# A state-space scan on Trainium2: GpSimd makes one of the four scalings of dt\*x by B in each step

## The chip, the cores and the metric

The kernel runs on one core of one Trainium2 chip. The metric is the device time of one execution in microseconds, the median of several runs. The core has five engines with a queue each, and a queue is worked off in order: TensorE (PE in the rows, its weight loads PEld), VectorE (DVE), ScalarE (ACT), GpSimd (POOL) and SyncE (SP), which issues DMAs. They are tied to each other by semaphores.

## What is computed

A layer of a sequence model: layernorm, a bidirectional state-space block, layernorm and sum, then attention and a mixture of eight experts. The change lies in the state-space block alone. Cut to that:

```
u: [2, 2048, 256];  x, z: [2, 2048, 512];  16 states per channel
xc = silu(causal_conv4(x));  dt, B, C = split(xc @ xp_w.T);  dt = softplus(dt @ dt_w.T + dt_b)
for t:                                       # forwards and, on flipped rows, backwards
    h = exp(dt[t] * A) * h + (dt[t] * xc[t]) * B[t]     # for each channel and state n
    y[t] = sum_n h[.., n] * C[t, n] + D * xc[t]
```

## The kernel before

The program is seven stages one after the other: projection of the inputs, the scan (`scan_channels`), mixing and qkv, attention, routing, the experts, and the combination. The change is in the scan.

The scan works in 16 units: two batches, four chunks of 512 positions, two directions. A unit holds 512 channels as four tiles of 128 partitions, and makes 16 steps, one per state n. A step is a chain over four engines:

- ACT scales the transposed product dt\*x (`dtxT`, positions on the partitions) by B for state n, four tiles of 128x512 (`spread_b`, L536 to L540), into `dBxT[n % 2]`; and makes four decays `dA = exp(dt * A)` (`decay`, L531 to L534). It works a step ahead of the scans: the scaling for step n+1 is queued at step n, and waits until PE has read the step that used the same buffer.
- PE transposes the scaled tiles back into PSUM (`inject`, L749 to L757), four transposes for each of the four channel tiles, into a ring of three banks `bx`.
- DVE runs the recurrence over 512 positions in one instruction per channel tile (`scan`, L661 to L672), from `dA` and `bx` into `hh[n % 2]`.
- POOL multiplies the result by C (L471), in two halves of two channel tiles each, into `hC[n % 2]`, and between them copies the last column of the scan into `state` (L469).
- PE adds the products to the accumulator (`add`, L759 to L768), eight channel tiles, that is two steps, behind the injects.

Between the steps of a unit the front of the next unit is made, in pieces placed by hand at fixed steps: the convolution on PE (L703) with its output on ACT (L485), the SiLU with two table loads on ACT (L490, L491, in step 3), the projections on PE (L713, L727) with their outputs on ACT (L498, L502, L510, L511), the softplus on ACT, POOL (L447, queued at step 9) and DVE (L644 and L650, after the scans of step 10), the product with x on DVE (L655, after step 11), and the transposes to `dtxT` on PE (L735) with their output on ACT (L529). All these pieces go through one PSUM bank `fr`, so PE and ACT take turns on it. PE's inject waits for ACT's scalings by the semaphore `bd_ok`.

Of the kernel before, what the change touches and what calls it, by code (L numbers as in the profile page):

```python
# [17 lines left out]
ALU = mybir.AluOpType  # L18
# [10 lines left out]
DT = DI // P  # L29
NS = 16  # L30
# [7 lines left out]
JT = C // P  # L38
# [92 lines left out]
def hold(eng, k):  # L131


    eng.sem_inc(k["passed"], 1)
# [207 lines left out]
def scan_channels(nc, k, xin, crows, y, convw, convb, xpw, dtw, dtb, alog, dskip):  # L342

    with Stage(nc, "scan") as s:
# [13 lines left out]
        dtxT = [s.sb(f"dtxT{i}", [P, JT, DI]) for i in range(2)]  # L358
# [3 lines left out]
        bt = [s.sb(f"bt{i}", [P, JT, 2 * NS]) for i in range(2)]  # L362
        dBxT = [s.sb(f"dBxT{i}", [P, JT, DI]) for i in range(2)]
# [8 lines left out]
        loaded_x = s.sems("loaded_x0", "loaded_x1")  # L372
        loaded_c = s.sems("loaded_c0", "loaded_c1")
        (loaded_w, diags, a_raw, a_ready, fr_mm, fr_out, silu_ok, e_ok, u_ok, v_ok, d_ok, ln_ok, dt_ok, front_ok,
         stored_c, bd_ok, bx_mm, da_ok, h_ok, hc_ok, saved, zeroed, acc_ok, skip_ok, y_out, y_stored) = s.sems(
            "loaded_w", "diags", "a_raw", "a_ready", "fr_mm", "fr_out", "silu_ok", "e_ok", "u_ok", "v_ok", "d_ok",
            "ln_ok", "dt_ok", "front_ok", "stored_c", "bd_ok", "bx_mm", "da_ok", "h_ok", "hc_ok", "saved", "zeroed",
            "acc_ok", "skip_ok", "y_out", "y_stored")
        NW = 7
        SUB = NS * DT  # L380
# [4 lines left out]
        FR_CONV, FR_PROJ, FR_BT, FR_DT, FR_NEXT, FR_TURN, FR_ALL = 0, 2, 3, 4, 8, 10, 14  # L385

        HELD_HC, HELD_H, HELD_SAVED, HELD_BX = 16, 8, 2, 8
        LAG = 8

        def bank(j):  # L390
            return 1 if j == SUB - 1 else j % 3

        def bank_free(j):
            back = 1
            while bank((j - back) % SUB) != bank(j):
                back += 1
            return j - back + 1 + HELD_H
# [7 lines left out]
        @block.sync  # L405
        def _(sp):
            for dst, src in ((cw[:, :, :, :], convw), (cb[:, :, :], convb), (db[:, :, :], dtb), (dk[:, :, :], dskip),
                             (an[:, :, :, :], alog), (wp[:, :, :, :], xpw), (wrk[:, :, :], dtw)):
                sp.dma_start(dst, src).then_inc(loaded_w, 16)

            def load_x(b, c, d):
                at = c * C if d == 0 else (NC - 1 - c) * C + HALO
                sp.dma_start(xw[d][:, :, :], xinv[b, :, :, at:at + C + HALO]).then_inc(loaded_x[d], 16)

            for d in range(2):
                load_x(0, 0, d)
            with sp.Fori(0, B) as b:
                for c in range(NC):
                    for d in range(2):
                        f = (b * NC + c) * 2 + d  # L420

                        sp.wait_ge(fr_mm, f * FR_ALL + 4)
                        hold(sp, k)
                        if c + 1 < NC:
                            load_x(b, c + 1, d)
                        else:
                            load_x(1 - b, 0, d)

                        sp.wait_ge(fr_out, f * FR_ALL + 5)
                        sp.dma_start(crows[d], pr[RANK:RANK + NS, :]).then_inc(stored_c, 16)  # L430
                        sp.wait_ge(stored_c, f * 16 + 16)
                        for g in range(NS // GROUP):

                            sp.wait_ge(hc_ok, (f * NS + g * GROUP - 2 * GROUP) * 2 + 2 * GROUP + HELD_HC)
                            sp.dma_start(cbc[g % 2][:, :, :],
                                         crows[d:d + 1, g * GROUP:(g + 1) * GROUP, :].broadcast_to([P, GROUP, C])
                                         ).then_inc(loaded_c[g % 2], 16)

        @block.gpsimd
        def _(pool):  # L440
            for i in range(2):
                pool.memset(hC[i][:, :, :], 0.0).then_inc(hc_ok, HELD_HC // 2)
            pool.sem_inc(saved, HELD_SAVED)

            def front_relu_and_e(d, g):
                pool.wait_ge(e_ok, g + 1)
                pool.tensor_tensor(dt[d][:, :, :], dt[d][:, :, :], ee[:, :, :], ALU.add).then_inc(v_ok, 1)  # L447

            front_relu_and_e(0, 0)
            with pool.Fori(0, B) as b:  # L450

                pool.wait_ge(saved, b * (2 * NC * NS) + HELD_SAVED)
                hold(pool, k)
                pool.memset(state[:, :, :, :], 0.0).then_inc(zeroed, 1)
                with pool.Fori(0, NC) as c:
                    for d in range(2):
                        f = (b * NC + c) * 2 + d
                        for n in range(NS):
                            q = f * NS + n
                            h, rows = hh[n % 2], cbc[n // GROUP % 2][:, n % GROUP, :]  # L460
                            edge = C - 1 if d == 0 else 0
                            if n % GROUP == 0:
                                pool.wait_ge(loaded_c[n // GROUP % 2], f * 32 + (n // GROUP // 2) * 16 + 16)
                            for half in range(2):
                                ms = slice(2 * half, 2 * half + 2)
                                pool.wait_ge(h_ok, q * DT + 2 * half + 2 + HELD_H)
                                if half:
                                    hold(pool, k)
                                    pool.tensor_copy(state[:, d, n, :], h[:, :, edge]).then_inc(saved, 1)  # L469
                                pool.wait_ge(acc_ok, q * DT + 2 * half + 2)  # L470
                                pool.tensor_tensor(hC[n % 2][:, ms, :], h[:, ms, :],  # L471
                                                   rows.unsqueeze(1).broadcast_to([P, 2, C]), ALU.mult
                                                   ).then_inc(hc_ok, 1)
                            if n == 9:
                                front_relu_and_e(1 - d, f + 1)

        @block.scalar
        def _(act):
# [55 lines left out]
                               ).then_inc(da_ok, 1)  # L534

            def spread_b(d, n):  # L536
                for j in range(JT):
                    last = act.activation(dBxT[n % 2][:, j, :], dtxT[d][:, j, :], ACT.Copy,  # L538
                                          scale=bt[d][:, j, NS + n:NS + n + 1])
                last.then_inc(bd_ok, 1)  # L540
# [30 lines left out]
            for m in range(DT):  # L571
                decay(0, 0, 0, m)
            act.wait_ge(fr_out, 14)
            spread_b(0, 0)

            def unit(b, c, d, f):
                o, g, first = 1 - d, f + 1, f * FR_ALL + 16
                for n in range(NS):
                    q = f * NS + n
                    dn, at = (d, n + 1) if n + 1 < NS else (o, 0)  # L580
                    if n + 1 == NS:
                        act.wait_ge(fr_out, first + FR_ALL)
                    act.wait_ge(bx_mm, q * DT + HELD_BX)
                    spread_b(dn, at)
                    if n == 2:
                        for half in range(2):
# [102 lines left out]
        def _(pe):  # L689
# [59 lines left out]
            def inject(d, f, j):  # L749
                n, m = j // DT, j % DT  # L750
                if m == 0:
                    pe.wait_ge(bd_ok, f * NS + n + 1)
                pe.wait_ge(h_ok, f * SUB + bank_free(j))
                for t in range(JT):
                    last = pe.transpose(bx[bank(j)][:, t * P:(t + 1) * P], dBxT[n % 2][:, t, m * P:(m + 1) * P],  # L755
                                        k["ident"][:, :])
                last.then_inc(bx_mm, 1)  # L757
# [1496 lines left out]
```

## Time and profile before

| | us |
|---|---|
| median of 3 runs | 4661.33 (4647.94 to 4668.38) |
| the profiled execution | 4669.25 |
| its span, first to last instruction | 4667.7 |
| busy in the span: PE, DVE, ACT, POOL | 3683.8, 2845.9, 2754.8, 1718.3 |

The page gives shares over the whole span, and the stages have different limits. The scan runs from about 248 to 2068 us of the span. What a change in it is worth is read from the rows of that stretch: which engine is busy in it, and which wait ends last before an instruction that stands idle. In the rows, "idle before" or a bracket is the idle time of the engine just before the instruction, with what ended it.

### The profile page before, as it was taken

How to read it: one execution, taken by the hardware profiler on the slowest of the kernel's cores; microseconds unless marked ns; L12 is line 12 of the kernel's file. 1: busy time of each engine (PE TensorE's matmuls, PEld its weight loads, DVE VectorE, ACT ScalarE, POOL GpSimd, SP SyncE). 2: the span in 40 equal slices, each digit the busy share in tenths (PEclk: the TensorE clock that was granted, in tenths of full speed). 3: DMA queues.
4: the chain of work that ended last, by engine and by line, in shares of the span. 5: the costliest groups of instructions: out<-in, count | busy, mean ns of one | idle time of the engine just before them, and what ended most of it. 6: DMA issues, size and time to landing. Idle time of an engine off the chain costs nothing. (4 is left out here: it accounts for less than half of the span.)

```text
span 4667.7 us, 68770 instructions
## 1 busy us (share of the span) xinstructions
PE 3683.8 (79%) x20726; PEld 2252.4 (48%) x20726; DVE 2845.9 (61%) x4186; ACT 2754.8 (59%) x4377; POOL 1718.3 (37%) x1132
## 2 busy tenths in 40 slices
PE   8488878888888888866776888888888885499990
PEld 4266666666666666644553222222222223366660
DVE  4268777787778777756665666666666665411105
ACT  3289898888989898964663455555555551011110
POOL 0067777777777777754342000000000002300006
PEclk9789999899989898988876899999999997699995
DMA  6311111111111111124544001000010103312215
GB/s 208 110 46 55 56 56 56 64 55 56 55 56 63 51 61 56 56 90 147 200 159 156 17 24 27 24 24 20 24 27 24 27 17 112 125 52 71 71 44 184
DMA packets 151517, 329.76 MB, mean 71 GB/s; under 512 B 17443, under 2 KB 92310, under 8 KB 136656
## 3 DMA queue, kind: packets, MB, share of 16 engines
q1 hardware_dynamic: 97392, 229.08, 14.5%
q10 hardware_dynamic: 39760, 51.81, 3.2%
q0 software_dynamic: 13968, 43.97, 2.8%
q8 instruction: 200, 3.28, 0.3%
q14 instruction: 197, 1.61, 0.1%
HBM read 216.45 MB, written 110.91 MB: 70 GB/s over the span
## 5 line engine op out<-in xcount | busy, mean ns | idle before, releaser
L671 DVE TENSOR_TENSOR_SCAN scan_hh<-scan_dA,scan_state,scan_bx 128x512 f32<-128x512 f32 x1024 | 1247.4, 1265 | 399.9 <-PE scan_bx L755 354.4
L471 POOL TENSOR_TENSOR scan_hC<-scan_hh,scan_cbc 128x1024 f32<-128x1024 f32 x512 | 1208.5, 2370 | 316.7 <-DVE scan_hh L671 243.1
L1403 DVE TENSOR_REDUCE attend_mx<-attend_s 128x1 f32<-128x512 f32 (+1 forms) x1360 | 782.3, 608 | 340.5 <-PE attend_s L1533 221.8
L755 PE MATMUL scan_bx<-kept_ident,scan_dBxT 128*128 128x128 f32 x4096 | 676.7, 291 | 151.2 <-DVE scan_hh L671 125.1
L755 PEld LDWEIGHTS scan_bx<-kept_ident,scan_dBxT 128*128 128x128 f32 x4096 | 521.3, 150 | 417.5 <-issue 209.4
L538 ACT ACTIVATE scan_dBxT<-scan_dtxT,scan_bt 128x512 f32<-128x512 f32 x1028 | 656.1, 712 | 89.4 <-PE scan_bx L755 89.2
L533 ACT ACTIVATE scan_dA<-scan_dt,scan_an 128x512 f32<-128x512 f32 x1028 | 655.5, 712 | 0.0
L765 PE MATMUL scan_acc<-kept_ident,scan_hC 128*128 128x128 f32 x4128 | 652.3, 286 | 1.3 <-POOL scan_hC L471 1.3
L1533 PE MATMUL attend_s<-attend_kt,attend_qt 96*128 96x512 bf16 (+1 forms) x1360 | 483.7, 374 | 145.6 <-DVE attend_mx L1403 74.3
L1497 ACT ACTIVATE attend_full<-attend_s 128x1024 f32<-128x1024 f32 x384 | 391.9, 1025 | 338.5 <-PE attend_s L1560 334.6
L765 PEld LDWEIGHTS scan_acc<-kept_ident,scan_hC 128*128 128x128 f32 x4128 | 521.7, 150 | 1.6 <-POOL scan_hC L471 1.6
L1381 POOL DMA_DIRECT2D scratch_attnT<-attend_out x16 | 7.9, 496 | 1341.1 <-DVE attend_out L1437 1341.1
L1533 PEld LDWEIGHTS attend_s<-attend_kt,attend_qt 96*128 96x128 bf16 x1360 | 129.5, 97 | 644.7 <-DVE attend_mx L1403 532.9
L703 PE MATMUL scan_fr<-scan_xw,scan_diag 128*128 128x512 f32 x560 | 303.6, 631 | 94.5 <-ACT scan_xc L485 39.0
L1560 PE MATMUL attend_s<-attend_qt,attend_kt 99*128 99x512 bf16 (+3 forms) x1284 | 360.7, 353 | 0.0
L1501 ACT ACTIVATE attend_diag<-attend_s 128x512 f32<-128x512 f32 (+3 forms) x512 | 192.7, 440 | 196.4 <-PE attend_s L1563 179.6
L2018 DVE TENSOR_TENSOR experts_yt<-experts_py,experts_b2t 128x256 f32<-128x256 f32 x64 | 27.2, 425 | 425.0 <-PE experts_py L2065 425.0
L2032 ACT ACTIVATE experts_hid<-experts_ph,experts_b1t 128x512 f32<-128x512 f32 x128 | 87.5, 687 | 249.8 <-PE experts_ph L2056 249.7
L2056 PE MATMUL experts_ph<-experts_xT,experts_w1t 128*128 128x512 f32 x512 | 224.7, 598 | 13.0 <-DVE experts_xT L2013 11.3
L2065 PE MATMUL experts_py<-experts_w2t,experts_hid 128*128 128x256 f32 x1024 | 222.3, 379 | 0.0
L2065 PEld LDWEIGHTS experts_py<-experts_w2t,experts_hid 128*128 128x128 f32 x1024 | 194.6, 190 | 29.9 <-issue 3.8
L1578 PE MATMUL attend_pv<-attend_full,attend_vs 128*32 128x512 f32 x1536 | 204.6, 605 | 0.0
(218 smaller groups left out, 4604.8 us busy)
## 6 DMA issues: line engine op xcount, KB each, us to landing
scan_cbc<-scratch_crows SPq DMA_DIRECT2D x64, 1024.0 KB, 4.7
scratch_qk<-mix_heads ACTq DMA_DIRECT2D x64, 384.0 KB, 9.7
scan_xw<-scratch_xin SPq DMA_DIRECT2D x18, 1030.0 KB, 7.3
scratch_y<-scan_uu ACTq DMA_DIRECT2D x17, 1024.0 KB
attend_qt<-scratch_qk SPq DMA_DIRECT2D x34, 384.0 KB, 3.9
attend_kt<-scratch_qk SPq DMA_DIRECT2D x34, 384.0 KB, 4.7
mix_yf<-scratch_y SPq DMA_DIRECT2D x10, 1024.0 KB, 8.4
mix_yb<-scratch_y SPq DMA_DIRECT2D x10, 1024.0 KB, 12.0
```

The lines of the kernel that those rows point to most:

```text
L471: pool.tensor_tensor(hC[n % 2][:, ms, :], h[:, ms, :], rows.unsqueeze(1).broadcast_to([P, 2, C]), ALU.mult).then_inc(hc_ok, 1)
L533: act.activation(dA[n % 2][:, m, :], dt[d][:, m, :], ACT.Exp, scale=an[:, d, m, n:n + 1]).then_inc(da_ok, 1)
L538: last = act.activation(dBxT[n % 2][:, j, :], dtxT[d][:, j, :], ACT.Copy, scale=bt[d][:, j, NS + n:NS + n + 1])
L671: dve.tensor_tensor_scan(hh[n % 2][:, m, r], dA[n % 2][:, m, r], bx[bank(j)][:, r], state[:, d, n, m:m + 1], ALU.mult, ALU.add).then_inc(h ...
L703: last = pe.matmul(fr[:, :], diag[:, d, m, j, :], xw[d][:, m, o:o + C], start=j == 0, stop=j == TAPS - 1)
L755: last = pe.transpose(bx[bank(j)][:, t * P:(t + 1) * P], dBxT[n % 2][:, t, m * P:(m + 1) * P], k["ident"][:, :])
L765: last = pe.matmul(acc[:, j, m * P:(m + 1) * P], hC[n % 2][:, m, j * P:(j + 1) * P], k["ident"][:, :], start=a == 0, stop=False, is_transp ...
L1403: dve.tensor_reduce(mx[:, t, c:c + 1], s1[v % 2][:, 0:w], AX_X, ALU.max).then_inc(s1_read, 1)
L1497: last = act.activation(buf[:, 2 * half:2 * half + 2, :], s2[st % 2][:, :, :], ACT.Exp)
L1533: last = pe.matmul(s1[v % 2][:, 0:w], qt[j1][0:STACK, t * P:(t + 1) * P], kt_[j1][0:STACK, c * C:c * C + w], start=True, stop=c < t // JT)
L1560: last = pe.matmul(s2[st % 2][:, r, o:], kt_[j][:, kt * P:(kt + 1) * P], qt[j][:, qc * C + o:(qc + 1) * C], start=True, stop=quad < qc)
L2065: last = pe.matmul(py[j % 2][:, :], hid[ch][:, f, (j % JT) * P:(j % JT + 1) * P], w2t[i][:, f, :], start=f == 0, stop=f == FT - 1)
```

## The change

Of the four tiles of `dBxT` in each step ACT makes three, and POOL makes the last (`JT - 1`), as a `tensor_scalar` of 128x512 with the column of B as its scalar. POOL queues it between its two products of a step, and for two steps ahead, while ACT queues its three for one step ahead. Before it POOL waits until PE has made all four injects of the step (the buffer is then free), and for the last two steps of a unit until the next unit's `dtxT` is there. The first two are made ahead of the loop. PE's inject waits for a second semaphore, `bd_pool`, beside `bd_ok`.

```diff
             front_relu_and_e(0, 0)
+            pool.wait_ge(fr_out, 14)
+            hold(pool, k)
+            for n in range(2):
+                spread_b(0, n)
             with pool.Fori(0, B) as b:
...
+            def spread_b(d, n):
+                pool.tensor_scalar(dBxT[n % 2][:, JT - 1, :], dtxT[d][:, JT - 1, :],
+                                   bt[d][:, JT - 1, NS + n:NS + n + 1], None, ALU.mult).then_inc(bd_pool, 1)
...
                                 pool.tensor_tensor(hC[n % 2][:, ms, :], h[:, ms, :],
                                                    rows.unsqueeze(1).broadcast_to([P, 2, C]), ALU.mult
                                                    ).then_inc(hc_ok, 1)
+                                if half == 0:
+                                    if n + 2 == NS:
+                                        pool.wait_ge(fr_out, f * FR_ALL + 16 + FR_ALL)
+                                    pool.wait_ge(bx_mm, (q + 1) * DT + HELD_BX)
+                                    hold(pool, k)
+                                    spread_b(d if n + 2 < NS else 1 - d, (n + 2) % NS)
...
             def spread_b(d, n):
-                for j in range(JT):
+                for j in range(JT - 1):
                     last = act.activation(dBxT[n % 2][:, j, :], dtxT[d][:, j, :], ACT.Copy,
...
                     pe.wait_ge(bd_ok, f * NS + n + 1)
+                    pe.wait_ge(bd_pool, f * NS + n + 1)
```

## Rows read from the trace of the kernel before

**Rows 1.** The page's engines over the whole span: busy us, share, instructions.

```profile
PE 3683.8 (79%) x20726; PEld 2252.4 (48%) x20726; DVE 2845.9 (61%) x4186; ACT 2754.8 (59%) x4377; POOL 1718.3 (37%) x1132
```

**Rows 2.** Stretches: one unit, and a run of ACT in it; the columns are the first line's.

```profile
core 0: us, PE busy (x) PEld busy (x) DVE busy (x) ACT busy (x) POOL busy (x), PEclk, DMA share, GB/s
929.26:1042.20 112.94, 96.00 (x616) 76.56 (x615) 88.88 (x68) 98.55 (x152) 83.96 (x49) 0.90 0.15 56
935.73:979.68 43.95, 36.86 (x274) 30.40 (x272) 34.08 (x28) 43.89 (x67) 33.70 (x22) 1.00 0.13 49
```

**Rows 3.** DVE's group L671, 300 to 1980 us; L469's durations min/median/max, whole span.

```profile
L671 DVE TENSOR_TENSOR_SCAN scan_hh<-scan_dA,scan_state,scan_bx 128x512 f32<-128x512 f32 x947 | 1153.5, 1265 | 346.6 <-PE scan_bx L755 304.2 <-ACT scan_dA L533 31.2 <-POOL scan_state L469 6.5
...
L469 POOL COPY scan_state<-scan_hh x256: 177/188/2289, 257.4 to 2065.5; 128x4 f32<-128x4 f32 x128
```

**Rows 4.** Waits, 300 to 1980 us: waiter, waited for: us in total, times, longest.

```profile
PE scan_fr L727 <- ACT scan_dt L511: 53.4, 29, 2.6
PE scan_fr L713 <- ACT scan_xc L490: 27.5, 14, 2.2
PE scan_bx L755 <- ACT scan_dBxT L538: 18.1, 23, 1.1
DVE scan_hh L671 <- ACT scan_dA L533: 31.2, 19, 4.8
```

**Rows 5.** Timeline: ACT in the run of rows 2, then DVE in steps 12 to 14.

```profile
935.73 2.56 ACT L538 ACTIVATE scan_dBxT<-scan_dtxT,scan_bt 128x512 f32<-128x512 f32 x4 [4.00 <-PE scan_bx L755]
...
973.53 1.94 ACT L538 ACTIVATE scan_dBxT<-scan_dtxT,scan_bt 128x512 f32<-128x512 f32 x3
...
1020.59 10.64 DVE L671 TENSOR_TENSOR_SCAN scan_hh<-scan_dA,scan_state,scan_bx 128x512 f32<-128x512 f32 x9
```

**Rows 6.** Timeline: PE and DVE where they stand behind ACT.

```profile
956.87 1.09 PE L713 MATMUL scan_fr<-scan_xc,scan_wp 128*96 128x512 f32 x2 [2.18 <-ACT scan_xc L490]
958.44 1.28 DVE L671 TENSOR_TENSOR_SCAN scan_hh<-scan_dA,scan_state,scan_bx 128x512 f32<-128x512 f32 x1 [1.59 <-PE scan_bx L755]
960.75 0.65 PE L755 MATMUL scan_bx<-kept_ident,scan_dBxT 128*128 128x128 f32 x4 [1.05 <-ACT scan_dBxT L538]
961.62 1.28 DVE L671 TENSOR_TENSOR_SCAN scan_hh<-scan_dA,scan_state,scan_bx 128x512 f32<-128x512 f32 x1 [1.90 <-PE scan_bx L755]
979.73 2.07 PE L727 MATMUL scan_fr<-scan_pr,scan_wrk 64*128 64x512 f32 x2 [2.16 <-ACT scan_dt L511]
982.88 1.28 DVE L671 TENSOR_TENSOR_SCAN scan_hh<-scan_dA,scan_state,scan_bx 128x512 f32<-128x512 f32 x1 [4.13 <-PE scan_bx L755]
```

**Rows 7.** Timeline: POOL and DVE from step 8 to the softplus of step 10.

```profile
989.12 2.36 POOL L471 TENSOR_TENSOR scan_hC<-scan_hh,scan_cbc 128x1024 f32<-128x1024 f32 x1 [2.29 <-DVE scan_hh L671]
1000.08 4.56 POOL L447 TENSOR_TENSOR scan_dt<-scan_dt,scan_ee 128x2048 f32<-128x2048 f32 x1
1004.58 2.39 POOL L471 TENSOR_TENSOR scan_hC<-scan_hh,scan_cbc 128x1024 f32<-128x1024 f32 x1
1004.74 4.37 DVE L644 SCALAR_TENSOR_TENSOR scan_ee<-scan_uu,scan_dt 128x2048 f32<-128x2048 f32 x1 [0.87 <-POOL scan_dt L447]
1006.88 2.28 POOL L469 COPY scan_state<-scan_hh 128x4 f32<-128x4 f32 x1
1009.12 2.34 POOL L471 TENSOR_TENSOR scan_hC<-scan_hh,scan_cbc 128x1024 f32<-128x1024 f32 x1
1009.22 4.40 DVE L650 SCALAR_TENSOR_TENSOR scan_dt<-scan_dtx,scan_ee 128x2048 f32<-128x2048 f32 x1
```

**Rows 8.** POOL's instructions by line over the whole span: busy us, mean ns.

```profile
L962 POOL TENSOR_TENSOR mix_rest<-mix_rot,mix_parts 128x512 f32<-128x512 f32 x32 | 36.9, 1153 | 171.4 <-DVE mix_parts L1070 171.4
L1375 POOL MEMSET attend_vs<- 128x512 f32 x2 | 1.1, 525 | 0.0
L120 POOL TENSOR_SCALAR_AFFINE_SELECT kept_ident<-kept_ident 128x128 f32<-128x128 f32 x1 | 0.3, 282 | 0.2 <-POOL kept_one L117 0.2
L112 POOL MEMSET kept_ident<- 128x128 f32 x1 | 0.2, 205 | 0.3 <-POOLq L2247 0.3
```

More of the change, by code:

```diff
@@ L374, in scan_channels @@
         (loaded_w, diags, a_raw, a_ready, fr_mm, fr_out, silu_ok, e_ok, u_ok, v_ok, d_ok, ln_ok, dt_ok, front_ok,
-         stored_c, bd_ok, bx_mm, da_ok, h_ok, hc_ok, saved, zeroed, acc_ok, skip_ok, y_out, y_stored) = s.sems(
+         stored_c, bd_ok, bd_pool, bx_mm, da_ok, h_ok, hc_ok, saved, zeroed, acc_ok, skip_ok, y_out, y_stored) = s.sems(
             "loaded_w", "diags", "a_raw", "a_ready", "fr_mm", "fr_out", "silu_ok", "e_ok", "u_ok", "v_ok", "d_ok",
-            "ln_ok", "dt_ok", "front_ok", "stored_c", "bd_ok", "bx_mm", "da_ok", "h_ok", "hc_ok", "saved", "zeroed",
+            "ln_ok", "dt_ok", "front_ok", "stored_c", "bd_ok", "bd_pool", "bx_mm", "da_ok", "h_ok", "hc_ok", "saved", "zeroed",
             "acc_ok", "skip_ok", "y_out", "y_stored")
```

## The prediction

> **What bounds the kernel now.** I read the page's table of engines first [rows 1]: TensorE is busiest over the whole span, but that is a mean over seven stages, and the change touches one, the scan. So the second view is the table of stretches [rows 2]. One unit of the scan (16 steps; 929.26 is the first scan of its step 0) takes 112.94 us, with ACT busy 98.6, PE 96.0, DVE 88.9 and POOL 84.0. There are 16 units, so 1 us per unit is 16 us of the kernel. No engine is full over a unit. The third view, the groups of the stage by line [rows 3], tells how they wait: DVE's scans lost 346.6 us, 304.2 of it to PE's inject (L755), 31.2 to ACT and 6.5 to POOL. The fourth, the waits [rows 4], asks what PE waits for in its turn. The rows where PE or DVE stands for ACT add up to 53.4 + 27.5 + 18.1 + 31.2 = 130.2 us in 300 to 1980, that is 14.9 units: 8.7 us per unit.
>
> The timeline of one unit shows where. ACT starts a run at 935.73, when PE frees the buffer, and does not idle until 979.68: 43.89 of 43.95 us busy [rows 2, 5]. In this run it makes seven steps' scalings and decays, and between them the conv output, the evacuation, the SiLU with two table loads, the projections. Three places hang on it [rows 6]: PE's projection waits 2.18 us for the SiLU (956.87), PE's inject of step 5 waits 1.05 us for the scaling (960.75), and PE's dt product waits 2.16 us for ACT's dt output (979.73), behind which DVE stands 4.13 us (982.88). So in steps 1 to 7 ACT sets the pace. From 985 on PE (the convolutions between injects) and POOL do, and in steps 12 to 14 DVE runs nine scans without a gap [rows 5].
>
> **The change, part by part.**
>
> *What ACT loses.* One of four scalings per step. A group of three lasts 1.94 us and one of four 2.56 [rows 5], so 0.61 us a step, 9.8 us a unit. It is worth something only where ACT is late. (a) From 935.73 to the scaling for step 5 there are four groups (for steps 2, 3, 4, 5): ACT comes 4 x 0.61 = 2.45 us earlier. The SiLU comes after three, 1.84 us earlier, against a stall of 2.18. The stalls behind them on DVE, 1.59 and 1.90 us before the scans at 958.44 and 961.62, hold that much: I take 2.4 us. (b) By the dt output seven groups have been saved, 4.3 us, of which 2.4 have been passed on in (a) already; the other 1.9 come off PE's stall of 2.16 at 979.73. Steps 5 and 6 in between are PE's and DVE's own, so the shift passes through unchanged. (a) and (b) are 4.3 us per unit. The rest of ACT's 9.8 falls in steps 8 to 15 and 0, where others end last: I cost it at nothing.
>
> *What POOL gains: the price p of one tensor_scalar, 128x512 f32.* The trace shows none. The nearest rows [rows 8]: a product of the same size with two inputs 1.153 us, a memset of that size, with no input, 0.525 us. A one-input instruction of 128x128 takes 0.282 us against 0.205 for the memset of that size; those 0.077 us, times four for the columns, on top of 0.525 give 0.83 us. I take 0.83, the one-input row being nearest in kind, with 0.53 and 1.15 as ends. The Trainium skill (GPSIMD Engine Reference) speaks against the change: its introduction calls GpSimd the wrong choice for ordinary elementwise arithmetic, and its section Performance versus the Vector engine has a tight loop over 512 elements at 769 ns. No row here shows that loop; by it the sum below would be better by 0.2 us per unit.
>
> *Whether POOL carries it.* POOL's 84.0 us become 84.0 + 16 x 0.83 = 97.3 of the new unit's 108 (102.4 with 1.15), so it becomes the busiest engine. A plain step costs it two products, a copy and p: 2 x 2.35 + 0.15 + 0.83 = 5.7 us, against 4.8 for DVE's four scans: in steps 12 to 14 POOL falls behind by 0.9 us a step. It may: the scaling is made two steps ahead. POOL's first product of a step can start after the step's second scan, and the inject that wants the scaling must be done six scans (7.2 us) later; less 0.65 for the inject and 3.2 for product and scaling, 3.3 us are in reserve. Three such steps use 2.7 of them, and step 0 (PE's convolutions) gives them back. The new wait for the injects (bx_mm) stands in POOL's queue before the scaling, the state copy and the second product; those need the same step's last two scans, which need the same injects, so it delays nothing that could have run. PE gets one more semaphore a step. For both I take 0.4 us per unit off.
>
> *Steps 8 to 10, where POOL is late already* [rows 7]. From 989.12 POOL makes steps 8 and 9 and the sum (L447, 4.56 us), for which DVE's subtraction (L644) waits. This one and the next (L650) read two SBUF tiles, take 4.37 and 4.40 us, and end 2.15 us after a POOL product ends (1006.97 and 1011.46); the state copy between them lasts 2.28 us where the median one lasts 0.19 [rows 3]. So these DVE instructions and POOL's exclude each other whole, and whichever stands waiting goes next. The Trainium skill (SBUF — State Buffer, Who interferes with whom) says the same: a VectorE instruction with two SBUF inputs and a GpSimd instruction that reads SBUF block each other for their whole length, and the order of issue decides who waits. The trace agrees, with the 2.28 us. Now L650 ends at 989.12 + 24.5. With the change: two steps of 4.85 + p, the sum 4.5, a product 2.35, L644 2.15, then the scaling (p) gets in ahead of L650 in place of copy and product (2.35), then 2.15: 20.85 + 3p. That is 23.3 for p = 0.83: 1.2 us gained (2.1 with 0.53, 0.2 with 1.15). The displaced product runs behind L650, 3 us later; PE needs it two steps on, so nothing waits.
>
> **Sum.** 2.4 + 1.9 + 1.2 - 0.4 = 5.1 us per unit, x 16 = 82 us. The profiled execution took 4669.25 us (span 4667.7 and 1.5 around it) and would take 4588; it lies 8 us above the median of the runs, 4661.33. On the median: 4580 us. The ends of p alone give 4.1 and 6.0 us per unit: 4596 and 4565.
>
> **Rivals.**
> 1. *All of ACT's time comes back.* Every stall behind ACT shrinks, the smaller ones too (conv output, decays). For: PE and DVE lose 8.7 us a unit to ACT. Against: steps 8 to 15. Bound 9.8 us per unit: 4505 us; around 4530 as a middle. 12%.
> 2. *The exclusion turns against it.* If the scaling starts just ahead of each of the three two-input DVE instructions of a unit, each waits p more and L650 gains nothing: 5.1 - 1.2 - 3 x 0.83 = 1.4 us, 22 us: 4639. For: POOL is nearly always in an instruction now. Against: at 1009 the scaling displaces a longer product. 10%. The Trainium skill's rule of issue order, named above, would make it so wherever the scaling is issued first.
> 3. *POOL sets the pace and eats the gain.* A lag in steps 11 to 15 that step 0 does not give back, p near 1.3: POOL's 84.0 + 21 = 105, plus 5 us in which it must wait for PE's adds and for ACT's exponential: 110 or more; gain 0 to 2 us: about 4650. For: 97 of 108 us busy in strict order. 12%.
> 4. *Slower: the price.* If the per-partition scalar makes p more than about 1.6 us, POOL's own 84.0 + 16p, with some 3 us of waits it cannot avoid, passes 112.9, and every unit takes what POOL takes. For p = 2.0: 119, 6 us per unit: 4760 us. For: no row shows this instruction. Against: it would cost more than the two-input product of its size [rows 8]. 12%.
> That leaves 54% for the forecast.
>
> **How the numbers follow.** About 0.5% (23 us) is what a measurement of this kernel can tell from no change. Faster: the forecast (54), rival 1 (12), some 5 of rival 2's 10 and 3 of rival 3's 12: 0.74. Same: the rest of those, 0.14. Slower: rival 4, 0.12. The range goes from 4530 (middle of rival 1) to 4645, which holds the forecast, both ends of p, rival 2 and part of 3; left out are rival 4, the far end of 1 and the upper end of 3, some 2 in 10.
>
> **What would show it.** Right: three scalings on ACT per step (1.94 us), 256 on POOL at 0.5 to 1.2 us; the waits of PE for the SiLU (27.5 us) and the dt output (53.4 us) at less than half; a unit of about 108 us, ACT near 89 us busy in it, POOL near 97; L650 shorter than 4.4 us. Wrong: waits of PE's inject for POOL's scaling, of DVE for POOL's copy or products, in sums of over 1 us a unit; a scaling above 1.3 us; the dt stall unchanged, which would mean that something other than ACT's queue held it.

## The result: slower by some 0.6 percent, and what the profile after shows

The changed kernel takes 4688.9 us (median; 4688.6 to 4698.3), the kernel before 4663.2 beside it: the ratio over all runs is 1.0067, 95% interval 1.0052 to 1.0081. The difference is small but clear of the noise. The forecast was 4580 with a range to 4645. The profiled execution has a span of 4687.6 us against 4667.7.

First GpSimd's new instruction by itself (minimum, median and maximum in ns, then its first and last start), with those who waited for it:

```profile
L450 POOL TENSOR_SCALAR scan_dBxT<-scan_dtxT,scan_bt x258: 1552/1574/3768, 235.0 to 2084.1; 128x512 f32<-128x512 f32 x129
...
  PE scan_bx L770: 54.0, 55
```

It lasts 1.55 us where nothing hinders it, and takes 1.51 from its start to the next instruction's. The forecast had 0.83, with 1.15 as its upper end. The stretches of two units (the second begins at the same place of the loop as [rows 2]; columns as there) and GpSimd's queue in the first, in which brackets would show idle time:

```profile
820.40:938.06 117.66, 92.11 (x611) 72.47 (x610) 90.43 (x67) 92.85 (x141) 112.98 (x67) 0.92 0.15 56
938.06:1048.94 110.88, 91.24 (x616) 72.70 (x615) 89.59 (x67) 89.79 (x136) 106.15 (x65) 0.95 0.16 58
```

```profile
823.59 1.55 POOL L450 TENSOR_SCALAR scan_dBxT<-scan_dtxT,scan_bt 128x512 f32<-128x512 f32 x1
825.10 0.18 POOL L477 COPY scan_state<-scan_hh 128x4 f32<-128x4 f32 x1
825.25 4.73 POOL L479 TENSOR_TENSOR scan_hC<-scan_hh,scan_cbc 128x1024 f32<-128x1024 f32 x2
829.97 1.55 POOL L450 TENSOR_SCALAR scan_dBxT<-scan_dtxT,scan_bt 128x512 f32<-128x512 f32 x1
...
888.65 2.36 POOL L479 TENSOR_TENSOR scan_hC<-scan_hh,scan_cbc 128x1024 f32<-128x1024 f32 x1
890.98 4.53 POOL L447 TENSOR_TENSOR scan_dt<-scan_dt,scan_ee 128x2048 f32<-128x2048 f32 x1
```

From 793.9 to 903.9 GpSimd has no idle time at all; a step costs it 6.34 us (scaling to scaling, 823.59 to 829.97 and on). It is busy 106 and 113 us of a unit, where before it had 84 of 113. ACT fell from 98.6 us busy to 90 to 93. VectorE at step 10 of the first unit, to be read against [rows 7]:

```profile
895.62 4.45 DVE L658 SCALAR_TENSOR_TENSOR scan_ee<-scan_uu,scan_dt 128x2048 f32<-128x2048 f32 x1 [4.41 <-POOL scan_dt L447]
900.17 5.91 DVE L664 SCALAR_TENSOR_TENSOR scan_dt<-scan_dtx,scan_ee 128x2048 f32<-128x2048 f32 x1
```

It waits 4.41 us for GpSimd's sum, where it had waited 0.87, and its second subtraction takes 5.91 us, where it had taken 4.40. Over 300 to 1980 us the waits (us in total, times, longest) that answer to [rows 4], and the new ones:

```profile
PE scan_fr L741 <- ACT scan_dt L525: 46.3, 30, 1.9
PE scan_fr L727 <- ACT scan_xc L504: 4.5, 7, 0.8
PE scan_bx L770 <- ACT scan_dBxT L552: 3.7, 8, 0.6
DVE scan_hh L685 <- ACT scan_dA L547: 27.3, 17, 2.0
DVE scan_ee L658 <- POOL scan_dt L447: 50.0, 15, 4.4
PE scan_bx L770 <- POOL scan_dBxT L450: 49.6, 51, 1.8
```

PE and VectorE stood 81.8 us for ACT, where it was 130.2: the stalls that the change aimed at did shrink. In their place stand 99.6 us for GpSimd, of which VectorE's wait for the sum had been 15.9 before, and PE's wait for GpSimd's scaling had not existed. TensorE's clock is no rival for the loss: over 300 to 1980 us its granted share rose (the last three figures are PEclk, DMA share and GB/s; before, then after):

```profile
300.00:1980.00 1680.00, 1378.30 (x9038) 1102.77 (x9038) 1316.97 (x992) 1489.86 (x2273) 1270.64 (x725) 0.92 0.16 57
300.00:1980.00 1680.00, 1341.15 (x8956) 1059.78 (x8957) 1318.58 (x984) 1339.55 (x2025) 1604.00 (x954) 0.94 0.15 57
```

Where in a unit that is, the starts of the first scan of each step tell. The table has the mean us of such stretches over 14 units (all but the first and the last), worked out from the traces, for the two kernels and for those of the experiments (e8 left out):

| | steps 1 to 4 | 5, 6 | 7 to 9 | 10 | 11 to 14 | 15, 0 | sum | median us |
|---|---|---|---|---|---|---|---|---|
| before | 25.2 | 13.5 | 23.2 | 15.5 | 22.0 | 14.3 | 113.7 | 4663 |
| after | 23.7 | 13.5 | 21.5 | 18.4 | 22.4 | 15.0 | 114.4 | 4689 |
| e1, fourth left out | 22.2 | 13.5 | 21.5 | 15.5 | 21.2 | 14.4 | 108.2 | 4583 |
| e2, load alone | 25.0 | 13.5 | 23.3 | 14.5 | 22.4 | 14.6 | 113.3 | 4679 |
| e3, two inputs | 22.4 | 13.5 | 22.2 | 14.0 | 21.2 | 14.2 | 107.4 | 4576 |
| e4, steps 2 to 8 | 22.8 | 13.5 | 22.3 | 15.5 | 21.9 | 14.0 | 110.0 | 4611 |
| e6, two inputs, 2 to 8 | 22.8 | 13.5 | 22.3 | 15.5 | 21.9 | 14.1 | 110.0 | 4612 |
| e7, not 12, 13 | 23.9 | 13.5 | 21.2 | 18.2 | 21.2 | 14.7 | 112.6 | 4657 |
| e9, after second | 24.9 | 13.5 | 21.3 | 17.7 | 25.0 | 14.2 | 116.6 | 4727 |
| e11, order | 23.8 | 13.5 | 21.2 | 15.7 | 23.7 | 14.7 | 112.7 | 4662 |
| e12, sum earlier | 23.7 | 13.5 | 21.6 | 15.0 | 24.3 | 14.8 | 112.9 | 4666 |
| e13, two inputs, sum earlier | 22.3 | 13.5 | 21.1 | 13.7 | 22.0 | 14.1 | 106.6 | 4560 |
| e14, padded | 24.2 | 13.5 | 21.2 | 19.8 | 22.4 | 14.4 | 115.5 | 4703 |

After against before: 1.4 us gained in steps 1 to 4, 1.8 in steps 7 to 9, 2.9 lost in step 10, 1.0 in 11 to 0; 0.8 us a unit lost in all. From the two spans: the scans, first to last, take 1827.2 us in place of 1816.4; the first starts 2.9 later; and GpSimd's last product ends 9.1 us after the last scan in place of 2.7. That is 10.8 + 2.9 + 6.4 = 20.1 of the 19.9 us between the spans. The 2.9 at the start is not seen in the trace of every later kernel and may be chance.

The column for steps 7 to 9 needs care, since TensorE's granted clock moves it. In the changed kernel, in e3 and in e13 each unit takes either 20.6 us there or 22.3 (one of each, from e3 and e13, columns as above):

```profile
1042.79:1065.09 22.30, 18.97 (x110) 13.99 (x109) 14.94 (x14) 19.84 (x29) 20.71 (x16) 0.92 0.28 97
1038.38:1059.00 20.62, 17.30 (x110) 12.32 (x109) 14.67 (x13) 18.16 (x29) 19.93 (x13) 1.00 0.32 105
```

The same 110 instructions keep PE busy 18.97 us in the first, in which the clock stood at its lower level (1.2 in place of 2.4 GHz) for 3.4 us, after PE had stood 1.94 us for ACT's dt output. Every unit of these kernels at a granted clock of 1.00 takes 20.6 us; one with a fall takes 20.6 or 22.3, as it seems by where it falls. Such units are 7 of 14 in the changed kernel, 13 in e3 and 4 in e13 at 22.3 us, so differences in this column between kernels with three scalings on ACT (21.1 to 22.2) are the clock's, not GpSimd's.

### The profile page after: what moved, and what is told of

It is laid out like the page before. It is cut to its first block and busy times, and to the rows that moved or that the text cites. A ratio compares the mean times of both kernels' runs of the same rounds, so it can differ in the third digit from the quotient of the medians.

```text
span 4687.6 us, 69557 instructions
## 1 busy us (share of the span) xinstructions
PE 3654.1 (78%) x20726; PEld 2213.3 (47%) x20726; DVE 2860.1 (61%) x4186; ACT 2601.7 (56%) x4120; POOL 2094.7 (45%) x1390
## 3 DMA queue, kind: packets, MB, share of 16 engines
q1 hardware_dynamic: 97392, 229.08, 14.5%
## 5 line engine op out<-in xcount | busy, mean ns | idle before, releaser
L770 PE MATMUL scan_bx<-kept_ident,scan_dBxT 128*128 128x128 f32 x4096 | 660.9, 286 | 263.5 <-DVE scan_hh L685 200.5
L770 PEld LDWEIGHTS scan_bx<-kept_ident,scan_dBxT 128*128 128x128 f32 x4096 | 504.0, 147 | 533.9 <-DVE scan_hh L685 352.7
L552 ACT ACTIVATE scan_dBxT<-scan_dtxT,scan_bt 128x512 f32<-128x512 f32 x771 | 498.6, 712 | 217.6 <-PE scan_bx L770 217.4
L780 PEld LDWEIGHTS scan_acc<-kept_ident,scan_hC 128*128 128x128 f32 x4128 | 507.3, 147 | 12.3 <-POOL scan_hC L479 7.2
L450 POOL TENSOR_SCALAR scan_dBxT<-scan_dtxT,scan_bt 128x512 f32<-128x512 f32 x258 | 447.5, 1735 | 15.5 <-ACT scan_dtxT L543 15.0
L2012 POOL DMA_DIRECT2D scratch_exp_out<-experts_yt x16 | 12.2, 760 | 486.8 <-DVE experts_yt L2033 486.8
```

What stands on the lines that cost most here:

```text
L450: pool.tensor_scalar(dBxT[n % 2][:, JT - 1, :], dtxT[d][:, JT - 1, :], bt[d][:, JT - 1, NS + n:NS + n + 1], None, ALU.mult).then_inc(bd_po ...
L780: last = pe.matmul(acc[:, j, m * P:(m + 1) * P], hC[n % 2][:, m, j * P:(j + 1) * P], k["ident"][:, :], start=a == 0, stop=False, is_transp ...
```

## The experiments

Two theories stood. PACE: the tensor_scalar is so dear that GpSimd's strict queue sets the pace. EXCLUSION: the harm is in where the scaling stands, at steps 10 and 11, next to VectorE's two-input instructions.

**e1_left_out.** Nobody makes the fourth scaling (the edit against the kernel before).

```diff
+            for i in range(2):
+                pool.memset(dBxT[i][:, JT - 1, :], 0.0).then_inc(bd_pool, 1)
...
-                for j in range(JT):
+                for j in range(JT - 1):
...
+            pe.wait_ge(bd_pool, 2)
```

> Leaves part of the computation out: nobody makes the fourth scaling (its quarter of the buffer is zeroed once), so ACT makes three a step as in the changed kernel and GpSimd has the load it had before. Two theories stand. PACE: a scaling costs GpSimd 1.51 us start to start, so a step costs it 6.34 us and it sets the pace; ACT's saving as such is worth what the prediction had, 4.3 us a unit: 4663 - 16 x 4.3 = 4594 us (4580 to 4605). EXCLUSION: the loss comes from the place of the scaling at steps 10 and 11, where GpSimd and VectorE's two-input instructions shut each other out; it gives about the same here. A third reading, that ACT's saving is worth little because PE and VectorE take over, gives 4640 or more.

Measured: 4583.1 us, 0.9844 of before (0.9825 to 0.9864). ACT's saving alone is worth 77 us by the medians (4.8 us a unit), and by the table, that is by one execution of each, 5.5 us a unit: 3.0 in steps 1 to 4, 1.8 in steps 7 to 9, 0.8 in 11 to 14. The forecast's 4.3 for (a) and (b) was a little low. Step 10 stays at 15.5. PACE and EXCLUSION expected the same here; the third reading falls.

Against e1 the loss of the changed kernel can be read part by part: ACT's saving gives 5.5 us a unit; GpSimd's load takes back 2.9 in step 10 and 3.3 outside it (1.5 in steps 1 to 4, 1.2 in 11 to 14, 0.6 in 15 and 0). What is left is the loss of 0.8 us a unit (by the unrounded figures).

**e3_two_inputs.** The same scaling by another instruction.

```diff
-                pool.tensor_scalar(dBxT[n % 2][:, JT - 1, :], dtxT[d][:, JT - 1, :],
-                                   bt[d][:, JT - 1, NS + n:NS + n + 1], None, ALU.mult).then_inc(bd_pool, 1)
+                pool.tensor_tensor(dBxT[n % 2][:, JT - 1, :], dtxT[d][:, JT - 1, :],
+                                   bt[d][:, JT - 1, NS + n:NS + n + 1].broadcast_to([P, DI]), ALU.mult
+                                   ).then_inc(bd_pool, 1)
```

> GpSimd makes the scaling as a product of two tensors, B broadcast along the free dimension, in place of a tensor_scalar. The kernel before has a two-input product of this size at 1.153 us. PACE: a step costs GpSimd 5.98 us in place of 6.34, it gains 5.9 us a unit on its work and reaches step 8 in time: the forecast's sum at p = 1.15, 4.1 us a unit, less 0.5 for start and end: 4605 us (4595 to 4640). EXCLUSION: as many GpSimd instructions stand between VectorE's two-input instructions as in the changed kernel, so the time stays within 10 us of its 4689.

Measured: 4576.3 us, 0.9831 (0.9810 to 0.9851): 113 us less than the changed kernel, with as many instructions at the same places. PACE had the direction, and its range ended 19 us too high; EXCLUSION as put, that the place and the number of the instructions make the loss, falls. GpSimd's instruction in this kernel, and the two engines at step 10:

```profile
L450 POOL TENSOR_TENSOR scan_dBxT<-scan_dtxT,scan_bt x258: 1029/1047/3107, 232.7 to 1967.4; 128x512 f32<-128x512 f32 x129
```

```profile
966.28 2.38 POOL L480 TENSOR_TENSOR scan_hC<-scan_hh,scan_cbc 128x1024 f32<-128x1024 f32 x1
966.45 4.37 DVE L659 SCALAR_TENSOR_TENSOR scan_ee<-scan_uu,scan_dt 128x2048 f32<-128x2048 f32 x1 [1.23 <-POOL scan_dt L447]
968.61 3.10 POOL L450 TENSOR_TENSOR scan_dBxT<-scan_dtxT,scan_bt 128x512 f32<-128x512 f32 x1
970.92 2.94 DVE L665 SCALAR_TENSOR_TENSOR scan_dt<-scan_dtx,scan_ee 128x2048 f32<-128x2048 f32 x1
971.66 2.25 POOL L478 COPY scan_state<-scan_hh 128x4 f32<-128x4 f32 x1
973.87 2.35 POOL L480 TENSOR_TENSOR scan_hC<-scan_hh,scan_cbc 128x1024 f32<-128x1024 f32 x1
```

1.03 us in place of 1.55. At step 10 the sequence of the prediction's part on steps 8 to 10 runs as written: product, first subtraction, scaling (held for 2 us), second subtraction, which now takes 2.94 us in place of 4.40, then copy and product. All 16 units have it, and step 10 is 1.4 us shorter than in e1. Against the changed kernel step 10 is 4.3 us shorter: VectorE waits 2.0 us less for the sum, and its two subtractions take 2.3 us less. So shutting out is still a part of the 113 us, by the order of the instructions and not by their number.

**e4_steps_2_to_8.** GpSimd makes the tensor_scalar for steps 2 to 8 alone.

```diff
+        BY_POOL = (2, 3, 4, 5, 6, 7, 8)
...
-                                if half == 0:
+                                if half == 0 and (n + 2) % NS in BY_POOL:
...
-                for j in range(JT - 1):
+                for j in range(JT - 1 if n in BY_POOL else JT):
```

> GpSimd makes the fourth scaling only for steps 2 to 8, where ACT was behind; ACT makes all four for the others. PACE: GpSimd carries 1.51 us more in seven steps that were longer than 6.34 us on the mean, catches up before step 10, and ACT's 4.3 us a unit stay: 4600 us (4590 to 4625). EXCLUSION: no scaling stands at steps 10 and 11, so the same. If neither: GpSimd's load in steps 0 to 6 alone puts it late at step 10, 4650 or more.

Measured: 4611.2 us, 0.9909 (0.9886 to 0.9931). Where GpSimd has room afterwards, even the dear instruction pays. Both theories had expected that; the reading that falls is that the load in steps 0 to 6 alone makes it late.

**e7_not_12_13.** As e4, with all steps but 12 and 13.

```diff
+        BY_POOL = (0, 1, 2, 3, 4, 5, 6, 7, 8, 9, 10, 11, 14, 15)
```

> GpSimd makes the fourth scaling for all steps but 12 and 13, which are the two queued between its products in steps 10 and 11, next to VectorE's two-input instructions; ACT makes four for those two. EXCLUSION: the loss of step 10 goes, 2.9 us a unit and more: 4600 to 4630 us. PACE: GpSimd still runs at 6.34 us a step from step 0 to 9 without idle time and reaches the sum late; only the two scalings less count, 1 to 2 us a unit: 4655 to 4675 us.

Measured: 4657.0 us, 1.0001 (0.9989 to 1.0014). With no scaling at step 10, that step still takes 18.2 us: VectorE waits for the sum, up to 4.6 us.

```profile
DVE scan_ee L659 <- POOL scan_dt L448: 53.7, 15, 4.6
```

PACE's 4655 to 4675 holds, and the loss at step 10 does not need the scaling there. Nor does e3's sequence come: in 15 of the 16 units the copy and the second product go ahead of the first subtraction, and the pair of subtractions takes 9.2 us.

**e8_prices.** A price list, from a single run.

```diff
...
+                if n % 8 == 0:
+                    made = pool.tensor_scalar(out[:, :], x, by, None, ALU.mult)
+                if n % 8 == 1:
+                    made = pool.tensor_scalar(out[:, :], x, 0.5, None, ALU.mult)
...
```

> A price list for GpSimd. ACT makes all four scalings as before, and GpSimd makes one more instruction at the place of the change into a spare buffer that nobody reads, in eight forms that alternate with the step: tensor_scalar with a per-partition scalar over 512, 256 and 128 columns, the same with a constant over 512, a product of two tensors over 512 with B broadcast, one with two full tensors, one broadcast over 256, and a copy over 512. COLUMNS: the tensor_scalar is dear for each column (1.51 us at 512, near 0.8 at 256, 0.45 at 128, the constant as dear). SCALAR: fetching the per-partition scalar is a fixed cost (512, 256 and 128 columns less than 0.5 us apart, the constant near 0.8). The product with a broadcast stays at 1.0 us start to start. Its time is of little use: between 4663 and 4740 us.

Measured: 4656.6 us (one run), below the expected range. The durations of the forms (ns, minimum, median, maximum; the larger ones were held up by VectorE):

```profile
L454 POOL TENSOR_SCALAR scan_spare<-scan_dtxT,scan_bt x33: 1553/1567/1602, 233.9 to 2043.3; 128x512 f32<-128x512 f32 x33
L456 POOL TENSOR_SCALAR scan_spare<-scan_dtxT x33: 1478/1490/1526, 235.4 to 2049.6; 128x512 f32<-128x512 f32 x33
L458 POOL TENSOR_SCALAR scan_spare<-scan_dtxT,scan_bt x32: 912/924/945, 258.6 to 1998.4; 128x256 f32<-128x256 f32 x32
L460 POOL TENSOR_TENSOR scan_spare<-scan_dtxT,scan_bt x32: 1029/1040/1068, 264.8 to 2004.5; 128x512 f32<-128x512 f32 x32
L462 POOL TENSOR_TENSOR scan_spare<-scan_dtxT x32: 1276/2310/3341, 272.8 to 2014.8; 128x512 f32<-128x512 f32 x32
L464 POOL COPY scan_spare<-scan_dtxT x32: 599/1652/2693, 278.8 to 2025.1; 128x512 f32<-128x512 f32 x32
L466 POOL TENSOR_TENSOR scan_spare<-scan_dtxT,scan_bt x32: 602/615/639, 284.1 to 2032.5; 128x256 f32<-128x256 f32 x32
L468 POOL TENSOR_SCALAR scan_spare<-scan_dtxT,scan_bt x32: 592/602/636, 291.3 to 2037.9; 128x128 f32<-128x128 f32 x32
```

COLUMNS holds: (1.553 - 0.912) / 256 = 2.5 ns for each column of the tensor_scalar, 128 to 512; a constant in place of the scalar saves 0.075 us, so SCALAR falls. The product with B broadcast costs (1.029 - 0.602) / 256 = 1.7 ns a column, the copy of 512 columns 0.60 us at best.

**e2_both.** GpSimd's load alone: its tensor_scalar goes to a spare buffer, ACT makes four.

```diff
-                pool.tensor_scalar(dBxT[n % 2][:, JT - 1, :], dtxT[d][:, JT - 1, :],
+                pool.tensor_scalar(spare[n % 2][:, :], dtxT[d][:, JT - 1, :],
...
-                for j in range(JT - 1):
+                for j in range(JT):
```

> GpSimd's load alone: it makes the tensor_scalar as in the changed kernel, with the same waits and PE waiting for it, but into a spare buffer, and ACT makes all four scalings as before. With ACT's three and no load on GpSimd the time was 4583 us, 77 below before. ADDITIVE: the load costs 25 + 77 us by itself: 4660 + 102 = 4762 us. PACE: GpSimd's 6.34 us a step and ACT's run are two limits of which the later counts, so ACT's fourth scaling adds only where GpSimd is not behind (step 4 and step 7, some 1.5 to 3 us a unit): 4710 to 4740 us.

Measured: 4679.3 us, 1.0038 (1.0026 to 1.0051). Both readings fail: the load costs 17 us, and taking a quarter of the scalings from ACT as well makes the kernel no faster (1.0067 of before against 1.0038). The table shows why. ACT's saving is there in the changed kernel (23.7 against 25.0 in steps 1 to 4, 21.5 against 23.3 in steps 7 to 9), but step 10 takes 18.4 us against 14.5. VectorE comes to it sooner, GpSimd does not: it is later by comparison, and VectorE waits 1.3 us a unit more for the sum. The larger part, 2.6 us, is the order of the instructions behind it. With the load alone the order at step 10 was e3's in all units (first subtraction, scaling, second subtraction: the good order from here on),

```profile
1004.96 4.37 DVE L659 SCALAR_TENSOR_TENSOR scan_ee<-scan_uu,scan_dt 128x2048 f32<-128x2048 f32 x1 [1.61 <-POOL scan_dt L448]
1007.15 3.61 POOL L451 TENSOR_SCALAR scan_spare<-scan_dtxT,scan_bt 128x512 f32<-128x512 f32 x1
1009.43 2.59 DVE L665 SCALAR_TENSOR_TENSOR scan_dt<-scan_dtx,scan_ee 128x2048 f32<-128x2048 f32 x1
```

and in the changed kernel in none. In 12 of its 16 units the scaling went ahead of the first subtraction (here at 784.00, not held up):

```profile
781.79 5.03 DVE L658 SCALAR_TENSOR_TENSOR scan_ee<-scan_uu,scan_dt 128x2048 f32<-128x2048 f32 x1 [2.17 <-POOL scan_dt L447]
784.00 1.55 POOL L450 TENSOR_SCALAR scan_dBxT<-scan_dtxT,scan_bt 128x512 f32<-128x512 f32 x1
786.92 4.40 DVE L664 SCALAR_TENSOR_TENSOR scan_dt<-scan_dtx,scan_ee 128x2048 f32<-128x2048 f32 x1
```

and in four, as in the unit of the result's section, the copy and the product went ahead of the second. The pair takes 7.1 us in the good order, 9.5 and 10.4 in these.

**e11_order.** The first subtraction ahead of the scaling by force, in the changed kernel.

```diff
                                     pool.wait_ge(bx_mm, (q + 1) * DT + HELD_BX)
+                                    if n == 10:
+                                        pool.wait_ge(d_ok, f + 2)
```

> The changed kernel with one wait more: at step 10 GpSimd makes its scaling only when VectorE's first subtraction of the softplus (L658) is done. In the changed kernel the two subtractions took 9.5 us together in 12 of 16 units and 10.4 in four, because the scaling or the copy and the second product went ahead of one of them; with the load alone (ACT making all four) the order was subtraction, scaling, subtraction in all units, and they took 7.1. ORDER: that order comes back by force, 2.4 to 3.3 us a unit: 4689 - 43 = 4646 us (4635 to 4665). PACE: GpSimd, which sets the pace, loses the 2 us for which it now waits, and gives the gain back in the steps behind: 4675 to 4695 us.

Measured: 4661.8 us, 1.0008 (0.9997 to 1.0020). What came is not quite the order of e2: both subtractions go ahead of the scaling, in all units, and the second has nothing in its way.

```profile
996.89 4.36 DVE L660 SCALAR_TENSOR_TENSOR scan_ee<-scan_uu,scan_dt 128x2048 f32<-128x2048 f32 x1 [2.47 <-POOL scan_dt L447]
1001.36 2.29 DVE L666 SCALAR_TENSOR_TENSOR scan_dt<-scan_dtx,scan_ee 128x2048 f32<-128x2048 f32 x1
```

Step 10 shrinks by 2.7 us to 15.7, and step 11 grows by 1.3: GpSimd, which had to wait, is later, and VectorE's product with x now takes 3.7 us in place of 2.4. So 27 us of the 43 stay, at the upper end of ORDER's range. The order has a share of its own in the loss, about as large as the whole loss, but it does not bring ACT's 77 us back.

**e12_sum_earlier.** The sum one step sooner.

```diff
-                            if n == 9:
+                            if n == 8:
                                 front_relu_and_e(1 - d, f + 1)
```

> The changed kernel with GpSimd's sum for the softplus (L447) queued after step 8 in place of step 9; ACT's exponential is done by then (881.26 in one unit, where the second product of step 8 starts at 882.32). LATE AT ONE PLACE: VectorE's wait for the sum, 50 us in 15 units, goes: 4689 - 16 x 3.3 = 4636 us (4620 to 4650). PACE: GpSimd's work of a unit is the same, and what it does sooner here makes its products late there: 4670 to 4695 us.

Measured: 4665.6 us, 1.0016 (1.0004 to 1.0028). VectorE no longer waits for the sum, and step 10 loses 3.4 us; steps 11 to 14 take 2.0 us more, and PE's wait for GpSimd's scaling grows from 49.6 to 111.0 us:

```profile
PE scan_bx L770 <- POOL scan_dBxT L450: 111.0, 85, 4.2
```

Between the two expectations: more than half of step 10's gain is given back in the steps behind. The order at step 10 is mixed here; in eight of the 16 units the two subtractions take 10.9 to 13.3 us together.

**e9_after_second.** The tensor_scalar behind the second product.

```diff
-                                if half == 0:
+                                if half == 1:
                                     if n + 2 == NS:
```

> The changed kernel with GpSimd's tensor_scalar queued after the second product of the step, not between the two; all else as it was. PLACE: if the loss came from holding up the state copy and the second product, it goes: 4600 to 4650 us. PACE: the same work in one strict queue, 6.34 us a step, and the scaling comes 2.5 us later for PE: 4685 to 4720 us.

Measured: 4726.9 us, 1.0134 (1.0109 to 1.0159). That is above both ranges. The place between the products was not the fault; the later one costs another 38 us, 2.7 us a unit of it in steps 11 to 14.

**e6_two_inputs_2_to_8.** e3's instruction for e4's steps.

```diff
+        BY_POOL = (2, 3, 4, 5, 6, 7, 8)
...
+                pool.tensor_tensor(dBxT[n % 2][:, JT - 1, :], dtxT[d][:, JT - 1, :],
...
+                                if half == 0 and (n + 2) % NS in BY_POOL:
```

> GpSimd makes the fourth scaling as a product of two tensors, and only for steps 2 to 8. Made for all steps it took 4576 us. If GpSimd, busy 96% there, was still a bound somewhere, leaving it nine steps less helps: 4560 to 4575. If every step's saving on ACT counted and step 10 gained from the scaling that stands between VectorE's two subtractions (14.04 us against 15.47 without it, in the two kernels run), it loses that: 4576 + 16 x 1.4 = 4598 us, up to 4605.

Measured: 4611.5 us, 0.9888 (0.9861 to 0.9914), the same as e4, and a little above the second reading. For these steps the price did not matter, and the nine others are worth 35 us with the cheap one, 1.4 a unit of it at step 10.

**e14_padded.** e3 made as dear as the change.

```diff
+                pool.tensor_tensor(spare[n % 2][:, :], dtxT[d][:, JT - 1, 0:DI // 2],
+                                   bt[d][:, JT - 1, NS + n:NS + n + 1].broadcast_to([P, DI // 2]), ALU.mult
+                                   ).then_inc(pad_ok, 1)
                 pool.tensor_tensor(dBxT[n % 2][:, JT - 1, :], dtxT[d][:, JT - 1, :],
...
+                                    pool.wait_ge(pad_ok, q + 1)
```

> The fourth scaling on GpSimd as a product of two tensors for all steps (4576 us), and ahead of each a second product of 256 columns into a buffer that nobody reads. In the price list such a product takes 0.556 us start to start and the scaling 0.982, together 1.54, against 1.51 for the tensor_scalar. PRICE: only the time on GpSimd counts: 4689 us as in the changed kernel (4670 to 4705). FORM: the tensor_scalar does harm in another way than by its length, as by the order at step 10: 4575 to 4640 us.

Measured: 4703.1 us, 1.0086 (1.0065 to 1.0106). With 0.56 us more on GpSimd in each step, e3's whole gain of 85 us turns into a loss of 37, and step 10 goes from 14.0 to 19.8 us. It is the time on GpSimd that does it, without any tensor_scalar. One thing is not kept apart: at step 10 the padding is also one instruction more that can go ahead of VectorE.

**e13_two_inputs_sum_earlier.** e3 with e12's edit.

```diff
+                pool.tensor_tensor(dBxT[n % 2][:, JT - 1, :], dtxT[d][:, JT - 1, :],
...
-                            if n == 9:
+                            if n == 8:
```

> The fourth scaling on GpSimd as a product of two tensors for all steps (4576 us), and the sum queued after step 8. VectorE waited 1.2 us a unit for the sum there. If only that wait goes: 4576 - 20 = 4556 us. If the scaling then falls before another of VectorE's two-input instructions and the order that was good at step 10 is lost: 4575 to 4600 us.

Measured: 4560.5 us, 0.9795 (0.9778 to 0.9812), the fastest of all, and near the first reading's 4556, but not by its mechanism. VectorE's wait for the sum is gone, yet step 10 gains only 0.4 us a unit: e3's good order is lost in all 16 units, and the two subtractions take 8.4 us in place of 7.4. Steps 11 to 14 give 0.8 back. What makes up the difference is steps 7 to 9, 1.1 us a unit or 18 us, and there it is TensorE's clock (four units at 22.3 us in place of 13). Whether the earlier sum brings the better clock about is not shown. GpSimd is busy 96% of the stretch from 300 to 1980 us in this kernel too:

```profile
300.00:1980.00 1680.00, 1411.62 (x9495) 1123.35 (x9494) 1377.94 (x1040) 1416.61 (x2140) 1605.65 (x1012) 0.95 0.17 61
```

## Why the prediction was wrong

- *What bounds the kernel, and (a) and (b).* Right. Steps 1 to 7 stood behind ACT; without any load on GpSimd (e1) steps 1 to 9 gave 4.8 us a unit, where the prediction had 4.3, and steps 11 to 14 another 0.8 that it had costed at nothing. In the changed kernel the waits for the SiLU fell from 27.5 to 4.5 us and those for the scaling from 18.1 to 3.7. The dt output was said to fall below half and fell only from 53.4 to 46.3, in slightly more but shorter waits. Step 7 shrank by 1.7 us, near the 1.9 of (b), yet not through this row: at a granted clock of 1.00 it went from 7.56 to 6.78 us, and the rest is the clock, 0.87 in the mean of step 7 before and 0.98 after. That the size of (b) came out is in part luck.
- *The price p.* This is the first step that failed: 1.51 us, where 0.83 was taken and 0.53 and 1.15 were the ends. The one-input row that was taken as nearest in kind [rows 8] was a select, and it was measured at 128 columns; neither its kind nor its step per column carried over. Taking a two-input product as the upper end rested on counting inputs. The price list shows that a tensor_scalar costs GpSimd half as much again as a two-input product with a broadcast.
- *The Trainium skill's figure.* The loop at 769 ns for 512 elements (GPSIMD Engine Reference, Performance versus the Vector engine), cited beside the sum, is half of what the tensor_scalar takes; here the measurement decides. The same page's introduction, cited against the change, sets GpSimd against VectorE; no run here puts the scaling on VectorE. On GpSimd the tensor_scalar lost, and e3's product, at 0.98 us from start to start, gained.
- *Whether POOL carries it.* The price alone does not turn the forecast: with p = 1.51 its sum is 2.4 + 1.9 - 0.9 - 0.4 = 3.0 us a unit, 48 us faster. The second step that failed is that GpSimd's lag was costed at 0.4 us. With p = 1.51 the prediction's own working gives 84.0 + 16 x 1.51 = 108.2 us, and a lag of 1.6 us a step in place of 0.9, for which the reserve (3.3 us, and 2.6 at this price) does not last three steps. The 0.4 us a unit that was taken off became 49.6 us of PE's waits in 14.9 units, 3.3; and the steps outside step 10 lost 3.3 us a unit against e1.
- *Steps 8 to 10.* Forecast a gain of 1.2 us, measured a loss of 2.9. With p = 1.51 the formula 20.85 + 3p gives a loss of 0.9. The rest has two sources: GpSimd came to step 8 late already, so that VectorE waited 2.3 us a unit more for the sum; and the rule that whichever stands waiting goes next does not hold in every unit, so that the two subtractions took 0.8 us more than before where the forecast had them shorter. Where the prediction's sequence does hold (e3), the step gained 1.4.
- *The rivals.* The second (the exclusion turns against it) came true at one of its three places: in 12 of 16 units the scaling went ahead of the first subtraction, which took 5.0 us in place of 4.4; the product with x stayed at 2.4. The third (p near 1.3, GpSimd sets the pace, about 4650) and the fourth (the price, from 1.6 us on) were the mechanism, and p fell between them; the fourth put the point of no gain too high. It came out of GpSimd's sum over a whole unit, as if no engine waited at one place for another's lateness. The kernel before had no reserve at step 10: VectorE waited 0.87 us there already [rows 7].

The chance of 12% for slower was too small for a term that no row showed and on which the terms of GpSimd hung.

What stays open: what decides who goes next at step 10. In the kernels with a late GpSimd (after, e14) the order was bad in every unit, in e7 in 15 of 16, and in e2 and e3 good in every unit; but VectorE's idle time before it overlaps (2.1 to 4.4 us in the changed kernel, 1.5 to 2.8 in e2).

## What to carry to other kernels

Price the instruction that is moved in its exact form on its new engine before anything else, and where no row shows it, give its price the width that a wrong guess of the kind would need: here 0.5 us decided between 85 us faster and 37 us slower. An engine with a strict queue should be asked at its latest point, the step at which another engine already waits for it, and not by its busy share over the loop: over 300 to 1980 us GpSimd was busy 1604.0 us in the changed kernel and 1605.7 in the fastest one. Taking work from one engine speeds up whoever waits for it, and so makes a third, unchanged engine late.

## What the hardware showed that was not expected

- On GpSimd a tensor_scalar of 128x512 in f32 takes 1.55 us, with a constant 1.48; a product with a broadcast column 1.03; a product of two full tensors 1.28; a copy 0.60.
- VectorE's two-input subtraction of 128x2048 takes 2.29 us when nothing is in its way (e11). A GpSimd product keeps it out whole: in e3 it ends 2.15 us after the scaling's end (971.71 and 973.86). A tensor_scalar does not: in e2 it ends 1.26 us after (1010.76 and 1012.02), so by these rows it runs beside the last microsecond of it (likewise in the unit of the changed kernel at 784.00: 785.55 and 786.82). The Trainium skill (SBUF — State Buffer, Who interferes with whom) has the loser wait for the full instruction; e3 agrees and e2 does not.
- When a product of GpSimd ends and both VectorE's subtraction and GpSimd's next instruction stand waiting, either may go first: in the changed kernel GpSimd's scaling did in 12 units and the subtraction in 4.
